# Products of two tiles in one VectorE instruction, and node comparisons moved to GpSimd, in the edge loop of a four-layer graph network

## The chip, the cores and the metric

The kernel runs on one core of one Trainium2 chip. The metric is the device time of one execution in microseconds, as the median of several runs.

## The reference, cut to what matters

Four graph layers follow each other on 1250 nodes with 512 features and 21250 edges (sorted by receiver). Each is added to its input and normalised. The change lies in the second layer, an equivariant message-passing layer, whose edge part is this:

```python
s0 = x0[sender]; s1 = x1[sender]                  # gathered rows: 128 and 3 x 128 numbers an edge
p1 = w1 * s0 * y0                                 # w1..w4: 4 x 128 weights an edge, h @ W_mlp4
p2 = (w2 * s0)[:, :, None] * y1[:, None, :]       # y0, y1: 1 + 3 numbers an edge
p3 = w3[:, :, None] * s1 * y0[:, None, :]
p4 = w4 * jnp.einsum('eum,em->eu', s1, y1) / SQRT3
msg0 = jax.ops.segment_sum(m0, receiver, num_segments=num_nodes)   # m0 = [p1, p4], m1 = [p2, p3]
msg1 = jax.ops.segment_sum(m1, receiver, num_segments=num_nodes)
```

## The kernel before, in words

The edges were sorted by the kernel itself into 208 tiles of 128 edges (`NT = G * GT`, 52 x 4). All edges of a tile have their receivers within one block of 32 nodes (`DB`). The edge loop walks over the tiles in steps of eight (`TP`): the loop body holds two steps (`par` 0 and 1), and there are 26 steps. All engines run their own stream and meet in semaphores.

For one tile m:

- GpSimd gathers the 128 sender rows of `xup` (512 numbers each) by an indirect DMA into slot m of `ring` (line 721, semaphore `s_gath[m]`). Before each step it copies the step's edge records into `gidx` and `gslot` (lines 710 and 711). Every second gather waits for `s_prod_ok`, that is until the products of the step before have left the two slots.
- TensorE computes the weights of two tiles at once, a pair (`tpw`, line 1102), into two PSUM banks: 0 and 1, or 6 and 7. `tpw` of a pair waits until the products two pairs earlier have read those banks.
- VectorE multiplies (`products`): line 2071 makes 2 x 128 products a lane, line 2072 makes 2 x 384 products a lane, from PSUM and `ring` into slot m mod 4 of `prod`. For every fourth tile it first compares the receivers of four tiles with 0 to 31 (line 2063, `eq4`).
- ScalarE scales the comparison result by the four y of each edge (line 1578, four instructions a tile, `sel4`).
- TensorE sums the tile's products by receiver with `sel4` as weights (`scat`, line 1116) into bank 2 + m mod 4. It waits for the tile's products and its `sel4`.
- VectorE adds the sum to the accumulator of the tile's node block (`add_sums`, line 2080). The block's number comes from a packed word which VectorE's sequencer loads once in four tiles (line 2090).

`add_sums` waits for two things: for its tile's `scat`, and for the addition of the tile before, because both may hit the same block of the accumulator:

```python
dve.wait_ge(s_scat_done, n + 5)
dve.wait_ge(s_gsum_ok, n + 4)
```

The order on VectorE before is: products of tile m + 3, addition of tile m, products of tile m + 4, addition of tile m + 1, and so on (`AHEAD = 3`). On TensorE it is, for each pair k: `tpw` of pair k + 1, then the two `scat` of pair k. Nothing of the rest of the kernel lies beside this loop: before it the node rows `xup` are written, and behind it TensorE waits for `s_acc_done`.

## Time and profile before

| | |
|---|---|
| median of 3 runs | 1691.36 us (1691.3 to 1697.8) |
| span of the profiled execution | 1690.4 us |
| PE busy | 1478.5 us |
| DVE busy | 1306.6 us |
| ACT busy | 739.0 us |
| POOL busy | 498.2 us |

The profiled execution is known by its span, 1690.4 us; the fastest of the three timed runs is 0.9 us longer than that, and the median 1.0 us. Busy time counts an engine's own instructions; the registers, waits and branches of its sequencer are not in it. Start times in the trace are counted from the span's start.

### The profile page before, as it was taken

The page shows a single profiled execution, that of the slowest core. Times are in us where ns is not written, and L with a number is a line of the kernel's source. Part 1 is how long each engine was busy: PE and PEld are TensorE (multiplying, and loading weights), DVE is VectorE, ACT ScalarE, POOL GpSimd, SP SyncE. Part 2 cuts the span into 40 slices and gives each one's busy share as a digit, 9 for nine tenths or more (in the row PEclk, how much of TensorE's full clock was granted, in tenths as well). Part 3 has the DMA queues.
Part 4 walks back from the last instruction along what each step waited for, and adds up shares of the span by engine and source line. Part 5 has one row for each costly group of instructions (what it writes and reads, how often), then busy time and mean ns, then how long its engine had stood idle before and what let it go on. Part 6 is the DMA issues. An engine that isn't in the chain of part 4 may idle for free.

```text
span 1690.4 us, 24268 instructions
## 1 busy us (share of the span) xinstructions
PE 1478.5 (87%) x7869; PEld 805.5 (48%) x7869; DVE 1306.6 (77%) x2051; ACT 739.0 (44%) x1580; POOL 498.2 (29%) x496
## 2 busy tenths in 40 slices
PE   2888998367888787899999999979999999999997
PEld 1465445213333335566555565855544444444443
DVE  8786999997999997499898999697577656632232
ACT  1285666267555555355454555441244333402000
POOL 1788888710011012356555664000000000002000
PEclk9988999678999997799999999979999999999999
DMA  4101000143121102466565667000111201220000
GB/s 143 42 6 9 6 7 7 36 146 114 43 68 40 65 16 82 129 184 183 165 183 165 182 184 148 1 1 26 50 50 50 70 30 58 66 74 1 13 19 30
DMA packets 66890, 122.06 MB, mean 72 GB/s; under 512 B 12753, under 2 KB 31299, under 8 KB 66702
## 3 DMA queue, kind: packets, MB, share of 16 engines
q0 software_dynamic: 23408, 59.71, 14.1%
q1 hardware_dynamic: 41976, 57.57, 10.5%
q10 hardware_dynamic: 1446, 4.03, 0.7%
q8 instruction: 31, 0.51, 0.1%
q14 instruction: 29, 0.24, 0.1%
HBM read 105.85 MB, written 15.23 MB: 72 GB/s over the span
## 4 chain that ended last, share of the span: by engine, by line
PE 53%; DVE 16%; POOL 14%; issue 10%; ACT 4%; DMA 2%; DVEq 1%; ACTq 0%; POOLq 0%
PE PS L1240 18%; POOL recs L656 14%; PE PS L1116 8%; DVE arena L1923 6%; PE PS L1205 5%; PE PS L1306 5%; PE PS L1102 5%; DVE arena L1919 3%; ACT arena L1578 3%; PE PS L1291 2%; PE PS L1302 2%; PE PS L1167 1%; DVE cnt_d L1704 1%; DVE arena L2123 1%; PE PS L976 1%
## 5 line engine op out<-in xcount | busy, mean ns | idle before, releaser
L1240 PE MATMUL PS<-arena 128*125 128x512 f32 x640 | 275.0, 592 | 0.0
L656 POOL DMA_INDIRECT recs<-arena x170 | 244.3, 1437 | 89.9 <-issue 89.0
L1578 ACT ACTIVATE arena<-arena,gslot 128x32 f32<-128x32 f32 x832 | 185.1, 308 | 172.5 <-PE PS L1116 89.6
L1116 PE MATMUL PS<-arena 128*32 128x128 f32 (+1 forms) x3328 | 235.0, 311 | 16.2 <-issue 8.0
L721 POOL DMA_INDIRECT arena<-xup,gidx x208 | 197.5, 949 | 147.6 <-issue 69.9
L1116 PEld LDWEIGHTS PS<-arena 128*32 128x32 f32 x3328 | 176.9, 111 | 127.1 <-issue 68.6
L1028 PE MATMUL PS<-arena 125*128 125x512 f32 (+1 forms) x480 | 190.5, 534 | 44.1 <-DVE arena L1923 43.9
L2072 DVE TENSOR_TENSOR arena<-PS,arena 128x768 f32<-128x768 f32 x208 | 196.7, 946 | 0.0
L1240 PEld LDWEIGHTS PS<-arena 128*125 128x125 f32 x640 | 120.1, 188 | 154.6 <-issue 154.1
L1028 PEld LDWEIGHTS PS<-arena 125*128 125x128 f32 x480 | 86.0, 191 | 148.4 <-issue 78.0
L728 POOL CAST arena<-cnt_s 125x1250 f32<-125x1250 uint16 x10 | 12.5, 1302 | 473.1 <-PE PS L1240 473.1
L1523 ACT ACTIVATE arena<-arena,c 125x1250 f32<-125x1250 f32 x80 | 106.8, 1337 | 101.2 <-DVE arena L1919 101.1
L1919 DVE SCALAR_TENSOR_TENSOR arena<-arena,c 125x1250 f32<-125x1250 f32 (+1 forms) x100 | 137.9, 1381 | 1.4 <-DVE c L1928 0.7
L1102 PE MATMUL PS<-arena 64*128 64x512 f32 x416 | 122.4, 660 | 1.8 <-issue 1.8
L1923 DVE SCALAR_TENSOR_TENSOR arena<-arena,cnt_s 125x1250 f32<-125x1250 f32 x80 | 116.0, 1451 | 0.0
L2071 DVE TENSOR_TENSOR arena<-PS,arena 128x256 f32<-128x256 f32 x208 | 86.5, 416 | 25.8 <-remote 9.8
L1660 ACT ACTIVATE arena<-arena,cslot 128x2500 f32<-128x2500 f32 x16 | 38.1, 2383 | 131.0 <-DVE cslot L2178 131.0
L1407 ACT ACTIVATE arena<-PS 125x626 uint16<-125x626 f32 x104 | 70.1, 692 | 57.4 <-PE PS L882 40.2
L2232 DVE TENSOR_SCALAR arena<-PS,deg 125x512 f32<-125x512 f32 x10 | 7.5, 751 | 111.9 <-PE PS L1306 111.9
L2080 DVE TENSOR_TENSOR arena<-PS,arena 128x256 f32 x208 | 85.7, 412 | 8.7 <-remote 7.6
L1306 PE MATMUL PS<-arena 125*125 125x512 f32 x200 | 87.5, 592 | 0.0
L1205 PE MATMUL PS<-arena,x_sb 125*128 125x512 f32 (+2 forms) x280 | 86.7, 471 | 0.0
(341 smaller groups left out, 2149.9 us busy)
## 6 DMA issues: line engine op xcount, KB each, us to landing
arena<-in_spline_wT SPq DMA_DIRECT2D x16, 1024.0 KB, 5.4
arena<-uv_rows SPq DMA_DIRECT2D x14, 610.4 KB
arena<-h_rows SPq DMA_DIRECT2D x26, 256.0 KB
h_rows<-arena SPq DMA_DIRECT2D x24, 256.0 KB, 2.8
arena<-xup,gidx POOLq DMA_INDIRECT x208
recs<-arena POOLq DMA_INDIRECT x170
xup<-arena SPq DMA_DIRECT2D x10, 250.0 KB
out<-x_sb SPq DMA_DIRECT2D x10, 250.0 KB
```

Source lines behind the costliest of these rows:

```text
L656: pool.indirect_dma_start(out=recs, out_offset=bass.IndirectOffsetOnAxis(pos[:, c:c + 1], 0), in_=rec[:, c, :], in_offset=None).then_inc(s ...
L721: pool.indirect_dma_start(out=ring[:, m, :], out_offset=None, in_=xup, in_offset=bass.IndirectOffsetOnAxis(gidx[:, par, m:m + 1], 0))\
L1028: ins = t.matmul(PS[:, 3 * par + q, 0:n1 - n0], hs[:, sblk, par * C:par * C + 2 * C], wt[:, sblk % WR, n0:n1], start=(sblk == 0), stop=(sb ...
L1102: t.matmul(PS[:, tpw_bank[(2 * k + q) % 4], :], h3[r, buf, k * 128:(k + 1) * 128], w_m4[r, :], start=True, stop=True, tile_position=(q * H ...
L1116: ins = t.matmul(PS[quad * DB:(quad + 1) * DB, bank, o0 * MUL:o0 * MUL + w], sel4[:, s, v * DB:(v + 1) * DB], prod[:, s, c0 * MUL:c1 * MUL ...
L1205: ins = t.matmul(PS[:, b0 + q, 0:n1 - n0], w, P50[:, k, n0:n1], start=(k == 0), stop=(k == NB - 1))
L1240: return t.matmul(PS[:NP, y2_bank(half, b), :], lhs[:, (k * HB + b) * NP:(k * HB + b + 1) * NP], w[:, k * D:(k + 1) * D], start=(first and ...
L1306: ins = t.matmul(PS[:NP, b % 2, :], cnt50[:, k, b * NP:(b + 1) * NP], z_sb[:, k, :], start=(k == 0), stop=(k == NB - 1))
L1578: ins = A(sel4[:, s, y * DB:(y + 1) * DB], eq4[:, m // 4, s * DB:(s + 1) * DB], ACT.Copy, scale=gslot[:, par, c + R_Y + y:c + R_Y + y + 1])
L1919: v.scalar_tensor_tensor(dst, U, cc, V, ALU.add, ALU.max).then_inc(ok, 1)
L1923: v.scalar_tensor_tensor(dst, e, 1.0, cm, ALU.min, ALU.mult).then_inc(ok, 1)
L2072: v.tensor_tensor(pr[:, :, 1:4, :], w[:, 1:4:2, :].unsqueeze(2).to_broadcast([128, 2, 3, MUL]), xg[:, 1:4, :].unsqueeze(1).to_broadcast([1 ...
```

## The change

Three things change in the edge loop:

- `products` becomes `pair_products`: lines 2071 and 2072 now cover both tiles of a pair, 4 x 128 and 4 x 384 products a lane, with one pair of instructions for two tiles. VectorE's order becomes: products of pair k + 1, addition of tile 2k, addition of tile 2k + 1.
- The comparison leaves VectorE. GpSimd makes it, tile by tile, for all eight tiles of a step, behind the step's second gather, into `eq8`.
- The other edits use one counting semaphore where several stood (`s_xt_cp`, `s_xt_ps`, `s_cols_cp`, `s_cols_ps`) and delete helper functions that nothing calls.

```diff
-        eq4 = at(22700, [128, 2, 4 * DB])
+        eq8 = at(22700, [128, 2, TP * DB])
@@ GpSimd, in the loop over the eight gathers of a step
+                        if m == 1:
+                            for q in range(TP):
+                                ins = pool.tensor_scalar(eq8[:, par, q * DB:(q + 1) * DB], iota_dst[:, 0:DB],
+                                                         gslot[:, par, q * RW + R_DL:q * RW + R_DL + 1], None, ALU.is_equal)
+                            ins.then_inc(s_eq_ok, 1)
@@ ScalarE
-                if m % 4 == 0:
-                    act.wait_ge(s_eq_ok, n4)
+                if m == 0:
+                    act.wait_ge(s_eq_ok, group)
@@ VectorE
-            def products(m, par, n, n_pair, n_gath):
...
-                v.tensor_tensor(pr[:, :, 0, :], w[:, 0:3:2, :], xg[:, 0:1, :].to_broadcast([128, 2, MUL]), ALU.mult)
-                v.tensor_tensor(pr[:, :, 1:4, :], w[:, 1:4:2, :].unsqueeze(2).to_broadcast([128, 2, 3, MUL]),
-                                xg[:, 1:4, :].unsqueeze(1).to_broadcast([128, 2, 3, MUL]), ALU.mult).then_inc(s_prod_ok, 1)
+            def pair_products(k, par, n, n_gath):
+
+                m, s = 2 * k, 2 * k % 4
+                xg = ring[:, m:m + 2, :].rearrange("p t (q n) -> p t q n", q=4)
+                b0 = (0, 6)[k % 2]
+                w = PS[:, b0:b0 + 2, :].rearrange("p t (h g n) -> p t h g n", h=2, g=2)
+                pr = prod[:, s:s + 2, :].rearrange("p t (h q n) -> p t h q n", h=2, q=4)
                 dve.wait_ge(s_gath[m], n_gath)
-                dve.wait_ge(s_tpw_ps, n + (2 - m % 2))
+                dve.wait_ge(s_gath[m + 1], n_gath)
+                dve.wait_ge(s_tpw_ps, n + 2)
+                v.tensor_tensor(pr[:, :, :, 0, :], w[:, :, :, 0, :], xg[:, :, 0:1, :].to_broadcast([128, 2, 2, MUL]), ALU.mult)
+                v.tensor_tensor(pr[:, :, :, 1:4, :], w[:, :, :, 1, :].unsqueeze(3).to_broadcast([128, 2, 2, 3, MUL]),
+                                xg[:, :, 1:4, :].unsqueeze(2).to_broadcast([128, 2, 2, 3, MUL]), ALU.mult).then_inc(s_prod_ok, 2)
@@ two_groups, VectorE
-                for m in range(TP):
-                    if m + AHEAD < TP:
-                        products(m + AHEAD, par, i * (2 * TP) + (TP * par + m + AHEAD), None, i * 32 + 16 * (par + 1))
+                for k in range(GT):
+                    if k + 1 < GT:
+                        pair_products(k + 1, par, i * (2 * TP) + (TP * par + 2 * k + 2), i * 32 + 16 * (par + 1))
...
-                    add_sums(m, i * (2 * TP) + (TP * par + m), word)
+                    for m in (2 * k, 2 * k + 1):
+                        add_sums(m, i * (2 * TP) + (TP * par + m), word)
```

On VectorE, inside the loop body, these rows stood one after another before: the products of a tile (lines 2071 and 2072), the registers and the addition of another tile (line 2080), and the same again. PS is PSUM; `arena` holds `prod`, `ring` and the accumulator.

```order
L2071 TENSOR_TENSOR arena<-PS,arena 128x2x128 [waits s_tpw_ps]
L2072 TENSOR_TENSOR arena<-PS,arena 128x2x384
L2080 REGISTER_ALU [waits s_gsum_ok,s_scat_done]
L2080 REGISTER_ALU
L2080 ISA
L2080 TENSOR_TENSOR arena<-PS,arena 128x256
L2071 TENSOR_TENSOR arena<-PS,arena 128x2x128 [waits s_tpw_ps,s_gath5]
L2072 TENSOR_TENSOR arena<-PS,arena 128x2x384
L2077 REGISTER_ALU
L2080 REGISTER_ALU [waits s_gsum_ok,s_scat_done]
```

At the same place of the changed kernel the products are lines 2040 and 2041 and the addition is line 2049.

```order
L2041 TENSOR_TENSOR arena<-PS,arena 128x4x384
L2058 ISA
L2058 TENSOR_LOAD gpk
L2058 ISA x2
L2046 REGISTER_ALU
L2049 REGISTER_ALU [waits s_gsum_ok,s_scat_done]
L2049 ISA
L2049 TENSOR_TENSOR arena<-PS,arena 128x256
L2046 REGISTER_ALU
L2049 REGISTER_ALU [waits s_gsum_ok,s_scat_done]
L2049 REGISTER_ALU
L2049 ISA
```

Two additions now stand behind each other with only register rows between them, and the second one waits for `s_gsum_ok`, which the first one raises; before, two product instructions stood between two additions.

On GpSimd, in the first step of the loop body of the changed kernel, the gathers are line 713:

```order
L703 COPY gslot<-gld 128x128
L704 ISA
L711 REGISTER_ALU [waits s_xup_out1,s_gidx_ok,s_xup_out0]
L713 DMA arena<-xup,gidx 128x512 [waits s_prod_ok]
L713 DMA arena<-xup,gidx 128x512
L718 TENSOR_SCALAR arena<-iota_dst,gslot 128x32 x8
L711 REGISTER_ALU
L713 DMA arena<-xup,gidx 128x512 [waits s_prod_ok]
```

The eight comparisons (line 718) stand between the second and the third gather; the row of eight was not there before, and the rest of GpSimd's order is as it was.

## Rows read from the trace of the kernel before

**Rows 1.** The page, part 1: busy time, share of the span, instructions of each engine.

```profile
PE 1478.5 (87%) x7869; PEld 805.5 (48%) x7869; DVE 1306.6 (77%) x2051; ACT 739.0 (44%) x1580; POOL 498.2 (29%) x496
```

**Rows 2.** Windows: length, busy time of PE, PEld, DVE, ACT, POOL, PEclk, DMA.

```profile
886.00:912.00 26.00, 22.83 (x220) 13.62 (x217) 20.18 (x43) 10.73 (x48) 12.84 (x16) 0.87 0.48 139
...
938.00:964.00 26.00, 25.48 (x290) 15.75 (x288) 25.34 (x53) 14.22 (x64) 15.72 (x21) 1.00 0.64 185
```

**Rows 3.** Groups by line and shape, 690 to 1060: busy, mean ns, idle before.

```profile
L2072 DVE TENSOR_TENSOR arena<-PS,arena 128x768 f32<-128x768 f32 x208 | 196.7, 946 | 0.0
L1578 ACT ACTIVATE arena<-arena,gslot 128x32 f32<-128x32 f32 x832 | 185.1, 308 | 172.5 <-PE PS L1116 89.6 <-DVE arena L2063 67.0 <-remote 15.8
...
L2071 DVE TENSOR_TENSOR arena<-PS,arena 128x256 f32<-128x256 f32 x208 | 86.5, 416 | 25.8 <-remote 9.8 <-DMA arena<-xup,gidx 7.8 <-PE PS L1102 5.1
L2080 DVE TENSOR_TENSOR arena<-PS,arena 128x256 f32 x208 | 85.7, 412 | 8.7 <-remote 7.6 <-DVE arena L2080 0.7 <-PE PS L1116 0.4
...
L2063 DVE TENSOR_TENSOR arena<-iota_dst,gslot 128x128 f32<-128x128 f32 x52 | 14.5, 280 | 4.7 <-POOL gslot L711 4.7
```

**Rows 4.** Timeline of DVE, four tiles of the steady loop: start, duration, instruction.

```profile
732.96 0.28 DVE L2063 TENSOR_TENSOR arena<-iota_dst,gslot 128x128 f32<-128x128 f32 x1
733.16 0.42 DVE L2071 TENSOR_TENSOR arena<-PS,arena 128x256 f32<-128x256 f32 x1
733.49 0.94 DVE L2072 TENSOR_TENSOR arena<-PS,arena 128x768 f32<-128x768 f32 x1
734.36 0.41 DVE L2080 TENSOR_TENSOR arena<-PS,arena 128x256 f32 x1
734.69 0.41 DVE L2071 TENSOR_TENSOR arena<-PS,arena 128x256 f32<-128x256 f32 x1
...
735.89 0.41 DVE L2080 TENSOR_TENSOR arena<-PS,arena 128x256 f32 x1
736.41 0.42 DVE L2071 TENSOR_TENSOR arena<-PS,arena 128x256 f32<-128x256 f32 x1
...
739.47 0.28 DVE L2063 TENSOR_TENSOR arena<-iota_dst,gslot 128x128 f32<-128x128 f32 x1
```

**Rows 5.** Timeline of DVE, the last additions of the loop.

```profile
1056.30 0.41 DVE L2080 TENSOR_TENSOR arena<-PS,arena 128x256 f32 x1
1057.07 0.42 DVE L2080 TENSOR_TENSOR arena<-PS,arena 128x256 f32 x1 [0.36 <-DVE arena L2080]
1057.86 0.42 DVE L2080 TENSOR_TENSOR arena<-PS,arena 128x256 f32 x1 [0.36 <-PE PS L1116]
1058.65 0.42 DVE L2080 TENSOR_TENSOR arena<-PS,arena 128x256 f32 x1 [0.36 <-DVE arena L2080]
```

**Rows 6.** Timeline of PE, 904 to 912, behind a stall of its own.

```profile
905.11 1.13 PE L1102 MATMUL PS<-arena 64*128 64x512 f32 x4
906.17 1.96 PE L1116 MATMUL PS<-arena 128*32 128x256 f32 x32
908.06 1.13 PE L1102 MATMUL PS<-arena 64*128 64x512 f32 x4
```

**Rows 7.** Timeline of POOL, one step of eight tiles.

```profile
735.80 0.28 POOL L711 COPY gslot<-gld 128x128 f32<-128x128 f32 x1
736.96 0.97 POOL L721 DMA_INDIRECT arena<-xup,gidx  x1 [0.87 <-issue]
738.23 0.95 POOL L721 DMA_INDIRECT arena<-xup,gidx  x1 [0.30 <-issue]
739.97 0.94 POOL L721 DMA_INDIRECT arena<-xup,gidx  x1 [0.79 <-DVE arena L2072]
...
743.23 0.94 POOL L721 DMA_INDIRECT arena<-xup,gidx  x1 [1.06 <-DVE arena L2072]
...
746.50 0.95 POOL L721 DMA_INDIRECT arena<-xup,gidx  x1 [1.08 <-issue]
...
748.85 0.28 POOL L711 COPY gslot<-gld 128x128 f32<-128x128 f32 x1
```

**Rows 8.** Groups of POOL by shape, whole span.

```profile
L710 POOL COPY gidx<-gld 128x8 uint32<-128x8 uint32 x26 | 5.2, 199 | 39.6 <-DVEq L2052 39.5
...
L643 POOL TENSOR_SCALAR_AFFINE_SELECT upper<-upper 128x128 f32<-128x128 f32 x1 | 0.3, 282 | 0.0
```

**Rows 9.** VectorE's sequencer, loop branch: duration ns min/median/max, first and last start.

```profile
L2095 DVEq FUSED_REGOPS  x12: 62/63/70, 701.6 to 1009.0; - x12
...
L2095 DVEq COMPARE_BRANCH  x12: 50/56/74, 736.9 to 1034.8; - x12
```

More of the change, by code:

```diff
@@ L733, in _ @@
             t = nc.tensor
-            def transposes(src, ready, done, copied, banks, copied0=0):
-                for b in range(NB):
-                    if ready is not None:
-                        pe.wait_ge(*ready(b))
-                    if b >= 2:
-                        pe.wait_ge(copied, copied0 + b - 1)
-                    for k in range(KT):
-                        ins = t.transpose(PS[:, banks[b % 2], k * 128:k * 128 + NP], src(b, k), ident[:NP, :NP])
-                    ins.then_inc(done, 1)
-            def node_product(lhs, rhs, nk, done, copied, banks, cols=D):
-                for b in range(NB):
-                    if b >= 2:
-                        pe.wait_ge(copied, b - 1)
-                    for k in range(nk):
-                        ins = t.matmul(PS[:NP, banks[b % 2], 0:cols], lhs(b, k), rhs(k), start=(k == 0), stop=(k == nk - 1))
-                    ins.then_inc(done, 1)
-            def blk_of(v):
-                return lambda b, k: v[:, k, b * NP:(b + 1) * NP]
             def uv_transposes(src, nr, done, b0):
@@ L1053, in x1_transposes @@
                     ins = t.transpose(PS[:, 4 + b % 2, k * 128:k * 128 + NP], src, ident[:NP, :NP])
-                ins.then_inc(s_xt1_ps, 1)
+                ins.then_inc(s_xt_ps, 1)
             def linear_up(b):
-                pe.wait_ge(s_xt1_cp, b + 1)
+                pe.wait_ge(s_xt_cp, NB + b + 1)
                 if b == 0:
@@ L1174, in _ @@
                 x2_transposes(b)
-            pe.wait_ge(s_xt2_cp, NB - 1)
+            pe.wait_ge(s_xt_cp, 3 * NB - 1)
             quad_rows(wa2, xT2, 0, 0, s_r4_ps)
             quad_rows(wa2, xT2, 1, 1, s_r4_ps)
-            pe.wait_ge(s_xt2_cp, NB)
+            pe.wait_ge(s_xt_cp, 3 * NB)
             quad_rows(wa2, xT2, 2, 2, s_r4_ps)
@@ L1282, in _ @@
             for c in range(NB):
-                pe.wait_ge(s_xt3_cp, c + 1)
+                pe.wait_ge(s_xt_cp, 3 * NB + c + 1)
                 if c == 0:
@@ L1320, in ln_sqrt, with evac_T @@
                 A(rstd[:, b:b + 1], mv[:, b, 1:2], ACT.Sqrt, bias=epsc[:NP, :]).then_inc(s_ln_sd, 1)
-            def evac_T(dst, done, copied, banks, layer=0, then=None):
+            def evac_T(dst, done, copied, banks, n0, layer, then):
                 if layer:
@@ L1329, in evac_T @@
                         ln_sqrt(layer, b + 1)
-                    act.wait_ge(done, b + 1)
+                    act.wait_ge(done, n0 + b + 1)
                     A(dst[:, :, b * NP:(b + 1) * NP],
@@ L1569, in _, with scaled_onehots @@
             A(w_o0[:, 1, :], w_o0[:, 1, :], ACT.Copy, scale=3.0 ** -0.5).then_inc(s_wo_ok, 1)
-            def scaled_onehots(m, par, n, n4):
+            def scaled_onehots(m, par, n, group):
                 s, c = m % 4, m * RW
-                if m % 4 == 0:
-                    act.wait_ge(s_eq_ok, n4)
+                if m == 0:
+                    act.wait_ge(s_eq_ok, group)
                 act.wait_ge(s_scat_done, n + 1)
                 for y in range(4):
-                    ins = A(sel4[:, s, y * DB:(y + 1) * DB], eq4[:, m // 4, s * DB:(s + 1) * DB], ACT.Copy,
+                    ins = A(sel4[:, s, y * DB:(y + 1) * DB], eq8[:, par, m * DB:(m + 1) * DB], ACT.Copy,
                             scale=gslot[:, par, c + R_Y + y:c + R_Y + y + 1])
```

61 lines of the change are left out of this document (19 added, 42 removed).

## The prediction

> **What bounds the kernel now.** The page's busy shares come first [rows 1]: TensorE 87%, VectorE 77%. They are means over stages, so they don't say who sets the pace of the edge loop; the views of the stretch from 690 to 1060 us do. In a steady window of 26 us VectorE is busy 25.34 us, at TensorE's full clock (1.00) [rows 2]. That window holds sixteen tiles. TensorE's busy time is as high, 25.48 us, but overlapping matmuls fill it, so I read its pace elsewhere. In the timeline of VectorE [rows 4] one instruction starts as the one before ends: from one comparison to the next, four tiles later, 739.47 - 732.96 = 6.51 us pass, of which about 0.2 us is idle. Behind a stall of its own, when it has work waiting, TensorE takes 908.06 - 905.11 = 2.95 us for a pair [rows 6], that is 5.90 us for four tiles. ScalarE is busy for 185.1 us of some 360 [rows 3]. So VectorE sets the pace with 6.51 us, TensorE is only 0.6 us behind it, and a gain on VectorE can be worth 0.6 us in four tiles at most, 52 x 0.6 = 31 us in all. In a few stretches TensorE stalls on itself and VectorE runs at 20.18 of 26 us [rows 2]; there the change is worth nothing. I count 5 of the 52 fours as lost to those and 47 as set by VectorE.
>
> **The pieces of VectorE's 6.51 us.** Starts matter here, not durations, since an instruction starts some 0.08 us before the one in front is over. From [rows 4]: 2071 to 2072 takes 733.49 - 733.16 = 0.33 us, 2072 to 2080 0.87, 2080 to 2071 734.69 - 734.36 = 0.33, comparison to 2071 0.20. Four tiles are 4 x 1.53 = 6.12, plus the comparison 0.20, plus one gap: between 735.89 and 736.41 there are 0.52 instead of 0.33, 0.19 more. Sum 6.51. I don't know the gap's cause for certain; the group view puts 5.1 us before 2071 down to `tpw` [rows 3].
>
> **The change, part by part.**
>
> *Longer products.* 256 elements take 0.33 us and 768 take 0.87: 0.54 us for 512 more, 1.05 ns an element, and so about 0.06 us fixed an instruction. A pair's first instruction has 512 elements, 0.33 + 0.27 = 0.60 us; the second 1536, 0.87 + 0.81 = 1.68. Together 2.28 against 2 x 1.20 = 2.40 before. The saving is 0.12 a pair, 0.24 in four tiles. The Trainium skill ("VectorE: DVE Perf Modes", on the errata mechanism) also says that many small tiles each pay a bubble which one large tile pays once.
>
> *Comparison gone from VectorE.* 0.20 us less in four tiles.
>
> *Two additions side by side.* Here the order shown above matters more than the instruction count. The second addition of a pair waits for the first one to be finished. Before, the products of another tile lay between, 1.20 us, and hid that wait: 2080 shows 0.7 us of waits for 2080 in the whole loop [rows 3]. The last additions of the loop, where no products are left, show the wait bare [rows 5]: starts at 1056.30, 1057.07, 1057.86, 1058.65, that is 0.77 to 0.79 us apart with 0.36 us idle, instead of 0.33. (The view names TensorE for one of the three; the distance is the same, so I read all three as the addition's own chain through the sequencer.) I take 0.78, so 0.45 more a pair, 0.90 in four tiles. Behind it on VectorE's queue stand the next pair's products, for which the gathers and TensorE's `scat` wait.
>
> A page speaks against this step. The Trainium skill ("VectorE: DVE Perf Modes", The DRAIN you can't avoid) measured a chain of copies as no slower with a semaphore behind each than with one at the end. By that rule the wait would be free, and the time would be that of the first rival below, 1666 us; these rows, in which the next instruction waits for that semaphore, show 0.36 us of idle time.
>
> *Sum for four tiles:* 6.51 - 0.24 - 0.20 + 0.90 = 6.97, with the gap of 0.19 kept. If the gap goes, 6.78. The gap is a wait for TensorE, which gets more room now, but I can't show that it goes: bounds 6.78 and 6.97, and I take 6.87. Against 6.51 that is +0.36 (+0.27 to +0.46), times 47: +17 us (+13 to +22).
>
> *The loop's branch.* Before, its sequencer work ran while products were under way. Now the loop body ends on an addition that was issued only just in time, so the branch and the registers behind it come ahead of the next products. Branch and register row take 0.056 + 0.063 = 0.12 us [rows 9], twelve times: +1.4 us. The lower bound is 0; for the upper I take the idle time that a late-issued addition shows, 0.36 us [rows 5], twelve times, 4.3 us. I take 2.
>
> *Entry and end.* The first products now wait for two gathers, which start 1.27 us apart when they don't wait (736.96 and 738.23, [rows 7]). So 0 to 1.3 us; VectorE waits later for TensorE at the entry anyhow, so I take 0. The last four additions were a chain before and still are: 0.
>
> *GpSimd's eight comparisons.* No row shows this operation. The nearest are a copy of 8 columns, 0.20 us, and a select of 128 columns, 0.28 us [rows 8]; 32 columns lie between, 1.6 to 2.3 us for eight. Is there room? A step takes 748.85 - 735.80 = 13.05 us, and the three waits in it are 0.79, 1.06 and 1.08 where a gather that doesn't wait shows 0.30 [rows 7]. Room is 0.49 + 0.76 + 0.78 = 2.0 us, and the work 11.0. At the new pace of 2 x 6.87 = 13.7 us there is 2.7, so up to 0.34 us each is hidden. The third and fourth gather of a step leave about 1 us later, but they are needed six tiles after their slot is freed, over 9 us. ScalarE needs the comparisons only once the step before has come to its fifth `scat`, some 6.9 us after the release of the first gather; two gathers (2.5) and 2.3 of comparisons are done by then. Cost 0. Without this cover it is the second rival.
>
> *TensorE.* `scat` of both tiles of a pair now starts at the end of the pair's products, then comes the next `tpw`: 2.95 us of work within a pair's 3.4. That hides with 0.4 us to spare. The merged semaphores and deleted helpers issue nothing in other places: 0.
>
> **Sum:** 17 + 2 = +19 us on the profiled execution, 1690.4 + 19 = 1709. The median of the runs lies 1.0 us above that span. I rounded the terms no finer than that, and predict 1710 us.
>
> **The rivals.**
>
> *The additions do not cost more* (the wait is overlapped, as the page's rule has it). Then four tiles need 6.87 - 0.90 = 5.97 on VectorE and 5.90 on TensorE: 0.54 less than 6.51, times 47 = -25 us, 1666 us. For it: the group view shows hardly any such wait. Against it: that view's additions stood apart, and three of three that stand together show it. It decides below a distance of 0.60 us between two additions: 0.33 + (6.51 - 5.97) / 2; above that the old 6.51 isn't undercut. Chance 0.12. Between the two, an extra of 0.1 to 0.3 us in place of 0.45, or a gap that vanishes along with less waiting than I think, gives 1683 to 1699: 0.20.
>
> *GpSimd becomes the bound.* If a comparison costs 0.5 us, a step is 11.0 + 4.0 = 15.0 us against 13.0: 26 x 2.0 = +52, 1743 us. For it: its instruction with a per-edge operand is shown nowhere. Against it: every small operation in its rows is under 0.3. It decides above 0.34 us. Chance 0.06.
>
> *More waits for TensorE.* The pair has one product instruction instead of two to be released, and the next pair's `tpw` lies behind both `scat`. If the gap came at each pair instead of each second one: another 0.19 x 47 = +9, and with the branch at its upper bound 1722 us. Chance 0.08.
>
> My own forecast, 1700 to 1717: 0.54.
>
> **How the numbers follow.** About 0.5%, 8.5 us, is what a measurement of this kernel tells from no change. Faster by more than that: the first rival and a small part of the cases between, 0.15. Within 0.5%, 1683 to 1700: most of the between cases and the lower edge of mine, 0.20. Slower: 0.65. The range leaves out the first rival and GpSimd's case (0.12 and 0.06): 1682 to 1726 us. The likeliest case alone is 1700 to 1717.
>
> **What the profile after would show.** VectorE: additions in twos, 0.78 us apart with some 0.36 us idle in the second, about 104 times, so close to 37 us of idle time before the addition, put down to the addition itself. Product instructions of about 0.68 and 1.75 us (start distances plus 0.08). Four tiles in 6.8 to 7.0 us. VectorE's busy time falls by 0.44 x 52 = 23 us although the span grows. GpSimd: comparisons of 0.2 to 0.28 us and gathers that still wait for the products. ScalarE: no waits for `s_eq_ok` in the steady loop. Wrong would be: additions 0.33 us apart, comparisons above 0.34 us, or a granted clock of TensorE that falls in the steady windows, for which nothing here gives a reason.

## The result, and the profile after

The changed kernel takes 1780.2 us (median of 4 runs, 1776.7 to 1785.1) beside 1692.6 us for the kernel before: ratio 1.052, interval 1.049 to 1.056, 88 us slower. Forecast were 1710 us, in a range of 1682 to 1726.

The page of the kernel after, part 1, on its profiled execution (span 1783.6 us), as in [rows 1]:

```profile
PE 1488.8 (83%) x7869; PEld 808.6 (45%) x7869; DVE 1288.7 (72%) x1791; ACT 746.8 (42%) x1580; POOL 575.6 (32%) x704
```

VectorE is busy 17.9 us less than before and the span is 93 us longer, so it waits more. For what, the groups of the loop say (690 to 1150 us, by shape, as in [rows 3]):

```profile
L713 POOL DMA_INDIRECT arena<-xup,gidx x208 | 200.4, 963 | 161.2 <-DVE arena L2041 96.4 <-issue 62.1 <-POOL gslot L703 2.7
...
L2041 DVE TENSOR_TENSOR arena<-PS,arena 128x1536 f32<-128x1536 f32 x103 | 180.1, 1749 | 0.0
...
L2049 DVE TENSOR_TENSOR arena<-PS,arena 128x256 f32 x204 | 85.8, 421 | 125.4 <-remote 93.5 <-DVE arena L2049 27.5 <-PE PS L1091 4.3
L2040 DVE TENSOR_TENSOR arena<-PS,arena 128x512 f32<-128x512 f32 x104 | 71.0, 683 | 23.0 <-DMA arena<-xup,gidx 16.9 <-remote 3.3 <-issue 2.5
```

The 27.5 us in which the addition (L2049) waits for itself were forecast. The 93.5 us were not; the view of the waits counts them as 26, which is about one for each of the 26 steps of eight tiles. "Remote" names no engine: the view found no instruction that had ended shortly before the wait did. The timelines of one stretch show what happened. First VectorE:

```profile
1010.64 0.42 DVE L2049 TENSOR_TENSOR arena<-PS,arena 128x256 f32 x1 [0.36 <-DVE arena L2049]
1010.99 0.68 DVE L2040 TENSOR_TENSOR arena<-PS,arena 128x512 f32<-128x512 f32 x1
1011.58 1.75 DVE L2041 TENSOR_TENSOR arena<-PS,arena 128x1536 f32<-128x1536 f32 x1
1013.25 0.42 DVE L2049 TENSOR_TENSOR arena<-PS,arena 128x256 f32 x1
1017.91 0.42 DVE L2049 TENSOR_TENSOR arena<-PS,arena 128x256 f32 x1 [4.24 <-remote]
```

A pair without a disturbance takes 3.38 us (from 1007.26, not shown, to 1010.64); this one takes 7.27. TensorE, whose `scat` (L1091) an addition waits for, in the same time (x is the number of instructions in a row):

```profile
1011.97 1.13 PE L1077 MATMUL PS<-arena 64*128 64x512 f32 x4
1013.46 0.97 PE L1091 MATMUL PS<-arena 128*32 128x256 f32 x15 [0.37 <-DVE arena L2041]
1014.72 0.27 PE L1091 MATMUL PS<-arena 128*32 128x128 f32 x1 [0.29 <-issue]
1015.43 0.38 PE L1091 MATMUL PS<-arena 128*32 128x256 f32 x1 [0.44 <-issue]
1016.14 0.62 PE L1091 MATMUL PS<-arena 128*32 128x256 f32 x4 [0.34 <-issue]
1017.56 1.60 PE L1091 MATMUL PS<-arena 128*32 128x128 f32 x11 [0.79 <-issue]
1019.09 2.08 PE L1077 MATMUL PS<-arena 64*128 64x512 f32 x4
```

The 16 `scat` matmuls of the second tile need 4.4 us instead of 1.0. Between them TensorE waits for nothing that the profile knows ("issue"): it starts one every 0.7 us. The `tpw` behind them takes 2.08 us instead of 1.13. In the window from 1018 to 1020 us the granted clock is 0.50, that is 1.2 GHz instead of 2.4; in the two windows of 2 us before, TensorE was busy for 1.08 and 1.06 us.

These starts are not yet what VectorE waits for. The addition that starts at 1017.91 needs the sums of a pair whose `scat` TensorE began at 1010.08 and, by the record, ended at 1012.03. But the ends of matmuls in the profile are modelled; the trace also holds the time of each semaphore signal, and there the signal of that `scat` stands at 1017.62, which is 5.6 us later. The `scat` of the tile before it was signalled at 1012.53, 1.4 us late, and none between the two. ScalarE, which waits for the same signals, starts at the same two moments:

```profile
1012.55 0.96 ACT L1553 ACTIVATE arena<-arena,gslot 128x32 f32<-128x32 f32 x4 [2.84 <-PE PS L1091]
1017.65 2.67 ACT L1553 ACTIVATE arena<-arena,gslot 128x32 f32<-128x32 f32 x12 [4.13 <-remote]
```

VectorE's own signals are on time in this stretch (product ends 1013.33, signal 1013.34). So it is TensorE that falls behind, and it does so before its starts show it. Of its 208 `scat` signals 26 come more than 4 us behind the recorded end. And GpSimd:

```profile
1003.94 0.97 POOL L713 DMA_INDIRECT arena<-xup,gidx  x1 [4.31 <-DVE arena L2041]
1005.22 0.95 POOL L713 DMA_INDIRECT arena<-xup,gidx  x1 [0.30 <-issue]
1006.20 2.72 POOL L718 TENSOR_SCALAR arena<-iota_dst,gslot 128x32 f32<-128x32 f32 x8
1009.08 1.04 POOL L713 DMA_INDIRECT arena<-xup,gidx  x1 [0.16 <-issue]
1010.42 0.94 POOL L713 DMA_INDIRECT arena<-xup,gidx  x1 [0.30 <-issue]
...
1014.18 0.94 POOL L713 DMA_INDIRECT arena<-xup,gidx  x1 [0.30 <-issue]
1015.43 0.95 POOL L713 DMA_INDIRECT arena<-xup,gidx  x1 [0.30 <-issue]
```

Eight comparisons in 2.72 us make it late. What its gathers wait for has then long happened, so six follow each other 1.25 to 1.34 us apart. Before, they mostly came in twos with a pause [rows 7]. TensorE's signals are late from the second of the six on (start 1010.42; the signal due at 1011.16 comes at 1012.53), its starts falter from the fifth on, and it recovers 1.2 us after the sixth has been issued. After a stall GpSimd waits for the slots to come free (4.31 us ahead of this step, 96.4 us in the loop), and the next step begins in the same way.

The kernel before has this too, where I had counted 5 of the 52 fours as lost without asking why. GpSimd and TensorE there (timelines; they lie in the first window of [rows 2], whose mean clock is 0.87):

```profile
888.62 0.94 POOL L721 DMA_INDIRECT arena<-xup,gidx  x1 [2.07 <-DVE arena L2072]
889.87 0.95 POOL L721 DMA_INDIRECT arena<-xup,gidx  x1 [0.30 <-issue]
...
896.13 0.95 POOL L721 DMA_INDIRECT arena<-xup,gidx  x1 [0.31 <-issue]
```

```profile
894.32 0.66 PE L1102 MATMUL PS<-arena 64*128 64x512 f32 x1 [0.47 <-issue]
895.73 1.01 PE L1102 MATMUL PS<-arena 64*128 64x512 f32 x1 [0.75 <-issue]
897.12 0.58 PE L1116 MATMUL PS<-arena 128*32 128x256 f32 x1 [0.39 <-issue]
```

Seven gathers 1.25 us apart, and TensorE starts one matmul every 1.4 us. Theory A was therefore: GpSimd's lateness makes a run of five or more gathers without a pause, and such a run slows TensorE. Rivals: B, the pair products; C, the comparisons as work of GpSimd's, wherever they stand; D, ScalarE waiting for their result. (The theories go by TensorE's starts, not by its signals.)

### The profile page after: what moved, and what is told of

It reads as the page before. It is cut to its first block, busy times and chain, and to the rows that moved or that the text cites. A ratio compares the mean times of both kernels' runs of the same rounds, so it can differ in the third digit from the quotient of the medians.

```text
span 1783.6 us, 24120 instructions
## 1 busy us (share of the span) xinstructions
PE 1488.8 (83%) x7869; PEld 808.6 (45%) x7869; DVE 1288.7 (72%) x1791; ACT 746.8 (42%) x1580; POOL 575.6 (32%) x704
## 4 chain that ended last, share of the span: by engine, by line
PE 43%; DVE 22%; POOL 13%; issue 12%; another core or an unknown queue 4%; DVEq 2%; DMA 2%; ACT 2%; POOLq 0%; ACTq 0%
PE PS L1215 17%; POOL recs L648 13%; DVE arena L2041 7%; DVE arena L1898 6%; PE PS L1091 6%; PE PS L1281 5%; PE PS L1180 5%; DVE arena L1894 3%; PE PS L1266 2%; PE PS L1277 2%; DVE arena L2049 1%; DVEq L2049 1%; PE PS L1142 1%; DVE cnt_d L1679 1%
## 5 line engine op out<-in xcount | busy, mean ns | idle before, releaser
L1091 PE MATMUL PS<-arena 128*32 128x128 f32 (+1 forms) x3328 | 241.3, 309 | 95.3 <-issue 48.8
L1553 ACT ACTIVATE arena<-arena,gslot 128x32 f32<-128x32 f32 x832 | 192.2, 311 | 255.8 <-PE PS L1091 129.1
L1091 PEld LDWEIGHTS PS<-arena 128*32 128x32 f32 x3328 | 184.1, 110 | 213.5 <-issue 122.2
L648 POOL DMA_INDIRECT recs<-arena x170 | 247.9, 1458 | 89.9 <-issue 89.3
L713 POOL DMA_INDIRECT arena<-xup,gidx x208 | 200.4, 963 | 161.2 <-DVE arena L2041 96.4
L2041 DVE TENSOR_TENSOR arena<-PS,arena 128x1536 f32<-128x1536 f32 x104 | 181.8, 1749 | 0.0
L2049 DVE TENSOR_TENSOR arena<-PS,arena 128x256 f32 x208 | 87.5, 421 | 126.5 <-remote 93.5
L2040 DVE TENSOR_TENSOR arena<-PS,arena 128x512 f32<-128x512 f32 x104 | 71.0, 683 | 23.0 <-DMA arena<-xup,gidx 16.9
```

The costliest lines, as they stand in the source:

```text
L648: pool.indirect_dma_start(out=recs, out_offset=bass.IndirectOffsetOnAxis(pos[:, c:c + 1], 0), in_=rec[:, c, :], in_offset=None).then_inc(s ...
L713: pool.indirect_dma_start(out=ring[:, m, :], out_offset=None, in_=xup, in_offset=bass.IndirectOffsetOnAxis(gidx[:, par, m:m + 1], 0))\
L1091: ins = t.matmul(PS[quad * DB:(quad + 1) * DB, bank, o0 * MUL:o0 * MUL + w], sel4[:, s, v * DB:(v + 1) * DB], prod[:, s, c0 * MUL:c1 * MUL ...
L1553: ins = A(sel4[:, s, y * DB:(y + 1) * DB], eq8[:, par, m * DB:(m + 1) * DB], ACT.Copy, scale=gslot[:, par, c + R_Y + y:c + R_Y + y + 1])
L2041: v.tensor_tensor(pr[:, :, :, 1:4, :], w[:, :, :, 1, :].unsqueeze(3).to_broadcast([128, 2, 2, 3, MUL]), xg[:, :, 1:4, :].unsqueeze(2).to_b ...
```

## Experiments

In the edits, "new" is the changed kernel and "old" the one before. Kernels of one group ran on one chip; ratios are against the kernel before on that chip.

**The two halves apart, and idle work** (kernel before: 1691.5 us).

`e1_pairs_only` is new with the comparisons on VectorE, one instruction for four tiles:

```diff
-  if m == 1:   # GpSimd, behind the second gather
-      for q in range(TP): ins = pool.tensor_scalar(eq8[...q...], iota_dst, gslot[...q...], None, ALU.is_equal)
+  if k % 2 == 0:   # VectorE, pair_products
+      v.tensor_tensor(eq8[... 4 tiles], iota_dst..., dl..., ALU.is_equal).then_inc(s_eq_ok, 1)
```

> The change's products of two tiles, but the comparisons back on VectorE, four tiles an instruction as before. Theory A (TensorE's slow stretches come from runs of back-to-back gathers, which GpSimd's 2.7 us of comparisons cause): no such runs, so few slow stretches, and only the forecast cost of the two additions side by side is left: 6.78 us for four tiles plus the comparison's 0.20, 1705 to 1718 us. Rival B (the stretches come from the pair products, since TensorE now waits for one long release instead of two): about 1780 us.

Measured: 1710.9 us, ratio 1.014 (1.008 to 1.020). No stall in every step. Its additions as forecast (timeline of VectorE):

```profile
946.51 0.41 DVE L2052 TENSOR_TENSOR arena<-PS,arena 128x256 f32 x1
947.28 0.42 DVE L2052 TENSOR_TENSOR arena<-PS,arena 128x256 f32 x1 [0.36 <-DVE arena L2052]
```

`e2_compare_only` is old with the eight comparisons on GpSimd, the products tile by tile as before:

```diff
-  VectorE: v.tensor_tensor(eq4..., ALU.is_equal)   # four tiles
+  GpSimd:  if m == 1: for q in range(TP): pool.tensor_scalar(eq8[...q...], ..., ALU.is_equal)
```

> The kernel before with only the comparisons moved to GpSimd, eight behind the second gather. Theory A: VectorE saves 0.2 us in four tiles, but the slow stretches of TensorE come, 50 to 90 us more than before: 1735 to 1775 us. Rival B: about 10 us faster than before, 1682 us.

Measured: 1768.9 us, ratio 1.047 (1.042 to 1.052). The large loss comes with the comparisons and not with the pairs: B falls.

`e4_idle_work` is old with its comparisons left on VectorE, and eight more on GpSimd that nobody reads:

```diff
+  if m == 1:
+      for q in range(TP): pool.tensor_scalar(eqd[...q...], iota_dst, gslot[...q...], None, ALU.is_equal)
```

> The kernel before, with eight comparisons more on GpSimd behind the second gather of each step, written to a tile that nobody reads; VectorE and ScalarE are as before. Theory A: the delay alone makes the runs of gathers and with them the slow stretches: 1740 to 1790 us. Rival D (it is ScalarE's or TensorE's dependence on GpSimd's comparison result that stalls): 1691 us, no change.

Measured: 1777.5 us, ratio 1.053 (1.048 to 1.059). D falls: nobody waits for these results.

`e3_spread` is new with two comparisons behind every second gather:

```diff
-  if m == 1: for q in range(TP): ...
+  if m % 2 == 1: for q in (m - 1, m): ...
```

> The changed kernel with the same 208 comparisons on GpSimd, but two behind every second gather instead of eight behind the second gather of a step. Theory A: 0.7 us fits in GpSimd's wait for products, gathers stay in twos, few slow stretches, 1700 to 1712 us. Rival C (it is the work of the comparisons on GpSimd as such, its total or its traffic, that slows the loop): about 1780 us, as the total is unchanged.

Measured: 1697.4 us, ratio 1.004 (1.002 to 1.007), a little below the forecast. As many comparisons, and 83 us less than new took in its own group. GpSimd's timeline shows why: no gather but the second of a pair follows without other work.

```profile
950.54 0.74 POOL L718 TENSOR_SCALAR arena<-iota_dst,gslot 128x32 f32<-128x32 f32 x2
951.44 1.04 POOL L713 DMA_INDIRECT arena<-xup,gidx  x1 [0.16 <-issue]
952.78 0.95 POOL L713 DMA_INDIRECT arena<-xup,gidx  x1 [0.30 <-issue]
953.75 0.73 POOL L718 TENSOR_SCALAR arena<-iota_dst,gslot 128x32 f32<-128x32 f32 x2
```

**The dose, and how much the gathers carry** (another chip; kernel before: 1689.8 us).

`e9_four_and_four` is new with four comparisons behind the second gather and four behind the sixth; `e10_idle_work_spread` is `e4_idle_work` with two idle comparisons behind every second gather:

```diff
e9:  -  if m == 1: for q in range(TP): ...
     +  if m % 4 == 1: for q in range(m - 1, m + 3): ...
e10: -  if m == 1: for q in range(TP): ...
     +  if m % 2 == 1: for q in (m - 1, m): ...
```

> The changed kernel, with four comparisons behind the second and four behind the sixth gather of a step. GpSimd is late by 4 x 0.36 = 1.4 us twice a step instead of by 2.9 once. Theory A: fewer gathers follow each other without a wait (three or so instead of six), so the stretches are rare: between the 1697 us of two by two and the 1780 of eight together, and nearer to the first, 1695 to 1720. Rival (each comparison costs TensorE something by itself, wherever it stands): 1765 to 1785.

Measured: 1705.7 us, ratio 1.008 (1.005 to 1.011). Up to four gathers stand in a row in it. Behind one such row of four (starts 743.43 to 747.27) TensorE's starts falter from 747.70 on and an addition waits 2.9 us; the additions' other waits are 2.35 us (at 907 us, behind another row of four) and under 1 us. So four in a row are not always harmless.

> The kernel before, in which GpSimd also does eight comparisons a step that nobody reads, two behind every second gather. The same work eight together behind the second gather took 1777.5 us. Theory A: the gathers keep their distance, the stretches are those of the kernel before, and GpSimd has no room left: 1688 to 1700 us. Rival (the work itself disturbs, by a port or by the instruction's kind): 1765 to 1785 us.

Measured: 1698.2 us, ratio 1.007 (1.004 to 1.010). The same work eight together cost 86 us, two by two 8 us. C falls.

`e5_narrow_gathers` is new, each gather fetching 64 of the 512 numbers of a row.

```diff
+  pool.memset(ring[:], 0.0)
-  pool.indirect_dma_start(out=ring[:, m, :], in_=xup, ...)
+  pool.indirect_dma_start(out=ring[:, m, 0:64], in_=xup.rearrange("n (a b) -> (n a) b", b=64), ...)
```

> The changed kernel, with the eight comparisons behind the second gather as it has them, but each gather fetches 64 of the 512 numbers of a row into the first eighth of its slot; the other numbers of the ring are zero from one memset before the loop (an estimate of 3.5 us). Left out: seven eighths of each gathered row, so the messages are not the reference's. GpSimd's instructions are as many and in the same order, so the gathers still follow each other six in a row behind the comparisons. Theory A (TensorE slows down because a run of gathers moves over 200 GB/s): the stretches with one TensorE instruction every 0.7 us are gone, and the time is that of the pair products alone or a little above, 1700 to 1715 us. Rival (it is the issuing of gathers back to back by GpSimd, or their descriptors, whatever they move): the stretches stay, 11 or so of them, 1770 to 1785 us.

Measured: 1786.3 us, ratio 1.055 (1.052 to 1.059). The theory as the expectation states it, that the moved bytes do it, falls. From the windows of this kernel (length, busy time of PE, PEld, DVE, ACT, POOL, PEclk, DMA share, GB/s), during one of its stalls:

```profile
967.00:969.00 2.00, 1.63 (x10) 0.47 (x8) 0.86 (x1) 0.00 (x0) 1.33 (x2) 1.00 0.47 137
969.00:971.00 2.00, 1.30 (x12) 0.48 (x8) 0.42 (x1) 0.75 (x4) 1.69 (x4) 1.00 0.09 16
```

TensorE starts 10 and 12 instructions in 2 us, where new starts 34 from 1010 to 1012 us, ahead of its stall, while the DMA engines move 137 and 16 GB/s; in the stall of new shown above, 1014 to 1016 us, they move 238 GB/s. It isn't the bytes.

**Which part of the run does it.** Three variants: `e12_run_broken` is new with two more idle comparisons behind the sixth gather; `e13_run_without_gathers` is new in which an addition of 128x512 numbers on GpSimd takes the place of gathers 3 to 8 of a step; in `e14_quarter_rows` each gather fetches 32 rows instead of 128, into a ring that was zeroed.

```diff
e12: +  if m == 5:
     +      for q in range(2): pool.tensor_scalar(eqd[...], iota_dst, gslot[...], None, ALU.is_equal)
e13: +  if m >= 2: pool.tensor_tensor(ring[:, m, :], gslot..., gslot..., ALU.add).then_inc(s_gath[m], 16)
e14: -  pool.indirect_dma_start(out=ring[:, m, :], ... gidx[:, par, m:m + 1] ...)
     +  pool.indirect_dma_start(out=ring[0:32, m, :], ... gidx[0:32, par, m:m + 1] ...)
```

> The changed kernel, all eight comparisons behind the second gather as it has them, and two more comparisons that nobody reads behind the sixth gather: GpSimd does more work than in the changed kernel (0.7 us a step), but its run of six gathers is now one of four and one of two. Theory A2 (TensorE slows down from the fifth gather of a run without a wait on, whatever the gathers carry): the stall of 3.6 us in every step goes, and GpSimd's own work, 8 x 1.27 + 10 x 0.36 + 0.5 = 14.3 us a step against some 14, becomes the limit: 1700 to 1725 us, faster than the 1780 of the changed kernel although it does more. Rival (the stall comes from GpSimd being 2.9 us late once a step, by itself): no better than 1780, rather 1785 to 1800.

> The changed kernel, in which GpSimd adds two vectors of 128x512 numbers of its own into the slots of tiles 3 to 8 of a step instead of gathering them (left out: three quarters of the gathers; those tiles' messages are not the reference's). GpSimd is as late and has a run of six instructions without a wait, but of arithmetic; an estimate of 0.6 to 1.2 us each. Theory A2 (the run of gather issues slows TensorE): no slow stretch in the loop, 1690 to 1712 us. Rival (GpSimd busy without a pause, whatever it does): a stall in every step, 1760 to 1785 us.

> The changed kernel, but each gather fetches the rows of the first 32 edges of its tile instead of all 128; the rest of the ring is zero from one memset before the loop (left out: the messages of three quarters of the edges). As many gathers in the same order, with a quarter of the descriptors each. If it is the descriptors that GpSimd writes (128 a gather, run of six) that slow TensorE, the stalls shrink or go: 1700 to 1730 us. If it is the number of gather instructions in a row, 1770 to 1785 us. An issue that is much shorter than 0.95 us would end the run of six as well, and is then the reason.

Measured: 1712.7, 1686.8 and 1693.5 us, ratios 1.030 (1.025 to 1.036), 1.014 (1.009 to 1.019), 1.019 (1.014 to 1.024), and no stalls in any of them. But the kernel before took 1661.7 us beside them instead of 1690. So new was run again beside them, on yet another chip (kernel before: 1663.0 us); c2, c3 and c4 are e12, e13 and e14 unchanged.

> The changed kernel once more, as the measure for the three that run beside it. In the last batch the kernel before took 1661.7 us instead of 1690, which is 28 us less; so it is open whether the stalls arise on every chip. Theory A2 (stall behind a run of six gathers, everywhere): ratio 1.05 and a stall of 3.6 us in every step. Rival (the stalls belong to some chips only): beside a kernel before of 1662 us it shows none, ratio 1.01 to 1.02; beside one of 1690 us it shows them, ratio 1.05.

> The run of six gathers broken by two idle comparisons, again, beside the changed kernel. If the changed kernel shows stalls here and this one none, and the time is lower although GpSimd does more (1710 to 1730 us beside 1780), the run of gathers is the cause. If both show stalls, or neither, this kernel doesn't tell it.

> Arithmetic in the place of six of eight gathers, again, beside the changed kernel (left out: those gathers; their tiles' messages are not the reference's). If the changed kernel shows stalls here and this one none (1685 to 1715 us beside 1780), it is the gathers and not GpSimd being busy without a pause. If it shows them too, it is GpSimd's business or its lateness.

> Gathers of 32 rows instead of 128, again, beside the changed kernel (left out: the messages of three quarters of the edges). The issue stays 0.88 us, and the run of six gathers stays. Stalls gone beside a changed kernel that shows them (1690 to 1715 us beside 1780): it is what the gathers' rows make, their descriptors or packets. Stalls there too: it is the instructions.

Measured: the changed kernel itself 1697.6 us, ratio **1.020** (1.016 to 1.025); the others 1711.1, 1684.9 and 1699.6 us (1.027, 1.011, 1.021). GpSimd and TensorE of the changed kernel on this chip:

```profile
946.47 1.04 POOL L713 DMA_INDIRECT arena<-xup,gidx  x1 [0.16 <-issue]
947.81 0.95 POOL L713 DMA_INDIRECT arena<-xup,gidx  x1 [0.30 <-issue]
...
951.57 0.95 POOL L713 DMA_INDIRECT arena<-xup,gidx  x1 [0.30 <-issue]
952.82 0.95 POOL L713 DMA_INDIRECT arena<-xup,gidx  x1 [0.30 <-issue]
```

```profile
950.37 1.95 PE L1091 MATMUL PS<-arena 128*32 128x256 f32 x32 [0.36 <-DVE arena L2041]
952.25 1.13 PE L1077 MATMUL PS<-arena 64*128 64x512 f32 x4
```

The same six gathers in the same rhythm, and TensorE does its 32 `scat` matmuls in 1.95 us; all 208 of its `scat` signals come 0.01 us behind the recorded end. So there are two kinds of chip here: on one (the result and the first two groups of experiments, kernel before 1690 to 1693 us) such a run stalls TensorE, on the other (1662 to 1663 us) it doesn't. Each chip was met in one group only, so "kind" may as well be a condition that a chip was in at that time; no run separates the two. These two groups say nothing on which part of the run stalls TensorE, and e12, the broken run, was never tried on the first kind. e13 and e14, as d1 and d2, then met a chip of the first kind (kernel before: 1690.1 us):

> Arithmetic of GpSimd in the place of six of eight gathers (left out: those gathers; their tiles' messages are not the reference's), once more, in the hope of a chip that shows the stalls: one on which the kernel before takes about 1690 us, not 1662. On two chips of the fast kind it and the changed kernel alike showed none. On a chip with stalls: if the gathers of the run make them, none here, 1690 to 1712 us, ratio 1.00 to 1.013. If GpSimd being late and busy without a pause makes them, one in every step, ratio 1.04 to 1.055. On a chip of the fast kind it tells nothing new (ratio 1.01).

> Gathers of 32 rows instead of 128 in an unchanged order (left out: the messages of three quarters of the edges), once more, in the hope of a chip that shows the stalls. There: if it is what the rows make (their descriptors, their packets, in all a quarter as many), no stall or a small one, 1690 to 1720 us, ratio 1.00 to 1.018. If it is the gather instructions in a row, which stay 1.17 us apart, a stall in every step, ratio 1.04 to 1.055. On a chip of the fast kind it tells nothing new (ratio 1.02).

Measured: without gathers in the run 1686.8 us, ratio 0.998 (0.997 to 1.000), no stall. With a quarter of the rows 1785.4 us, ratio 1.058 (1.056 to 1.060). TensorE's timeline in this second one, gathers 1.17 to 1.23 us apart from 940.0 to 943.6 and again from 945.2:

```profile
944.55 0.64 PE L1094 MATMUL PS<-arena 128*32 128x256 f32 x10 [0.37 <-issue]
945.62 0.60 PE L1094 MATMUL PS<-arena 128*32 128x128 f32 x4 [0.44 <-issue]
947.09 0.27 PE L1094 MATMUL PS<-arena 128*32 128x128 f32 x1 [0.86 <-issue]
947.83 0.27 PE L1094 MATMUL PS<-arena 128*32 128x128 f32 x1 [0.47 <-issue]
```

So neither bytes nor rows: what matters is that gather instructions follow each other. Two gathers alone already do a small part of it. d1 has only two in a step, at 945.70 and 947.05 here; the `scat` signal due at 947.02 comes at 948.61, 1.6 us late, the next ones are on time again, and 21 of its 208 signals are over 1 us late, none over 1.65. ScalarE shows it: in d1 it has to stop for that signal between the scalings of two tiles, while in c3, the same kernel on a chip of the second kind, all eight instructions behind the first gather (948.46) run in a row. ScalarE in d1:

```profile
946.31 0.96 ACT L1558 ACTIVATE arena<-arena,gslot 128x32 f32<-128x32 f32 x4 [1.67 <-PE PS L1096]
948.63 0.96 ACT L1558 ACTIVATE arena<-arena,gslot 128x32 f32<-128x32 f32 x4 [1.37 <-remote]
```

And in c3:

```profile
948.95 1.83 ACT L1558 ACTIVATE arena<-arena,gslot 128x32 f32<-128x32 f32 x8 [1.55 <-PE PS L1096]
```

On the first kind of chip, then, a pair of gathers puts TensorE 1 to 1.6 us behind, and in the pause behind the pair it catches up; six in a row leave it no time for that.

That GpSimd is late and busy isn't enough, with one reserve: its additions take 1.01 us each and not 1.25, so after four of them it had caught up and waited 0.5 to 0.8 us. It was busy for 6.8 us without a pause behind its second gather, against 10 in new.

**A better order of the pair.** `e8_additions_between` has the comparisons on VectorE as `e1_pairs_only`, and the order: long product, addition 2k, short product, addition 2k+1.

```diff
-  product 512; product 1536 (raises s_prod_ok); addition 2k; addition 2k+1
+  product 1536; addition 2k; product 512 (raises s_prod_ok); addition 2k+1
```

> Pair products, but the two additions of the pair before stand between and behind the two product instructions (long product, addition, short product, addition), and the comparisons are back on VectorE, four tiles in one instruction; GpSimd has gathers alone. If an addition waits 0.45 us only because it stands right behind the other one, that goes: VectorE needs 0.60 + 1.68 + 2 x 0.33 = 2.94 us a pair, 0.1 more for the comparisons, about 3.0, and TensorE's 2.95 is the next limit. Against the 3.26 of before: 0.25 less times some 94 pairs, 1666 to 1675 us. Rival 1 (the short product waits for the addition or the addition for the product on the way, 0.36 us as between two additions): no better than 3.3 a pair, 1690 to 1700 us. Rival 2 (a faster VectorE frees slots sooner, GpSimd's gathers bunch up and TensorE's slow stretches return): 1700 us or more, and the stretches would be seen behind runs of gathers without a wait.

Measured (first kind of chip, kernel before 1689.8 us): 1726.6 us, ratio 1.021 (1.018 to 1.024). This forecast missed by over 50 us. The additions waited for TensorE, 30.7 us by "remote" and 25.5 by name in the loop: an addition asks for sums whose `scat` has only just been released, and part of these signals are late as above (recorded end 945.94, signal 947.51, addition 947.80). `e11_additions_later` puts each odd addition one place later, behind the next pair's long product; it also waits for `s_scat_done` ahead of the long product, and its first step stands outside the loop:

```diff
-  product 1536 (k+1); addition 2k;   product 512 (k+1); addition 2k+1
+  product 1536 (k+1); addition 2k-1; product 512 (k+1); addition 2k
```

> As the kernel with the additions between the products, but each odd addition stands one place later, behind the next pair's long product (long product, odd addition of the pair before last, short product, even addition). There an addition did wait for TensorE, for 30.7 + 25.5 us in the loop, since its tile's sums had only just been asked for. If that was what cost, VectorE waits only for the slots of the products before the long one: 3.1 to 3.2 us a pair, 1675 to 1690 us. Rival (TensorE itself needs over 3.3 us a pair once it is asked this early, or ScalarE's copies behind the later comparison do): 1700 to 1730 us, no better than 1726.

Measured, on a chip of the second kind only: 1653.4 us beside 1661.7, ratio 0.996 (0.993 to 0.998). Its timeline of VectorE shows the pair in 2.93 to 3.2 us, without a wait between additions:

```profile
950.91 1.75 DVE L2044 TENSOR_TENSOR arena<-PS,arena 128x1536 f32<-128x1536 f32 x1
952.58 0.41 DVE L2056 TENSOR_TENSOR arena<-PS,arena 128x256 f32 x1
952.91 0.68 DVE L2048 TENSOR_TENSOR arena<-PS,arena 128x512 f32<-128x512 f32 x1
953.51 0.41 DVE L2056 TENSOR_TENSOR arena<-PS,arena 128x256 f32 x1
953.84 1.75 DVE L2044 TENSOR_TENSOR arena<-PS,arena 128x1536 f32<-128x1536 f32 x1
```

It is the only version here that does the reference's whole work and is faster than the kernel before on its own chip, by 8 us. `e8_additions_between` and this one never ran on the same kind of chip, so how much of their difference comes from the order, and how much from signals that are on time here, is not shown; nor was it tried where gathers stall TensorE.

## Why the prediction was wrong

**Longer products, additions side by side, the gap:** right. The products take 0.68 and 1.75 us, the additions stand 0.78 us apart with 0.36 idle, the gap of 0.19 has gone, a pair takes 3.38, so four tiles 6.76. The branch costs 0.34 us, not 0.12: once in sixteen tiles a pair takes 3.72 us. That is 4 us in the loop, near my upper bound, and 0.085 in four tiles, which gives 6.85; I had taken 6.87 without the branch. VectorE's busy time fell by 17.9 us, not 23.

The idle 0.36 us is not the semaphore's price. In all 105 such gaps of the loop of `c1_after_again` (37.3 us in the 103 that the view puts down to the addition) 0.04 us pass from the end of the first addition to the wait instruction of VectorE's sequencer, and 0.32 us from there to the start of the second addition, with three register instructions in between, which work out the block's address. They stand behind the wait. The view of the addition's line in the changed kernel lists them (DVEq is VectorE's sequencer; durations in ns):

```profile
L2049 DVEq ALU_OP  x364: 40/45/57, 709.7 to 1154.0; - x182
L2049 DVEq FUSED_REGOPS  x208: 57/57/57, 709.8 to 1154.1; - x104
```

So the case doesn't contradict what the Trainium skill measured ("VectorE: DVE Perf Modes", The DRAIN you can't avoid): a semaphore behind each copy costs nothing extra there, and here 0.04 of the 0.36 us. What didn't hold was my step from there to the first rival. Working the address out ahead of the wait might save most of the 0.32 us; no run here tries it.

**"GpSimd's eight comparisons ... Cost 0":** this step failed, in three places. First the price: 0.36 us each (359 ns over 208), not 0.20 to 0.28, and above my own limit of 0.34, one of the listed signs of being wrong. Second the timing: "the third and fourth gather of a step leave about 1 us later" looked at two gathers. The third starts 3.86 us behind the second instead of 1.74 [rows 7], and since GpSimd doesn't catch up before the step ends, all six go out without a pause. Third, and this is the cost: I asked only when the gathers are needed. On this kind of chip the gathers themselves slow TensorE, and a run of six without a pause puts it 5 us behind; the prediction had no term for that, neither here nor under TensorE, whose work it let hide "with 0.4 us to spare". None of its rivals named it, and the one on GpSimd priced lateness by its busy time, 1743 us at 0.5 us each. Two more of its signs failed. ScalarE does wait for the comparisons in the loop (73.6 us in 25 waits in `c1_after_again`), though the additions wait for TensorE for only 0.8 us there, so it cost VectorE next to nothing. And the granted clock does fall, to 0.50 behind some of the stalls.

**What the terms measured.** On chips without stalls the change costs 34.6 us (1697.6 - 1663.0; by the interval of the ratio 26 to 41) where 19 were forecast. Chips of the two kinds differ by 82.6 us for the changed kernel (1780.2 - 1697.6) and by 29.6 for the one before (1692.6 - 1663.0), so stalls cost it 53.0 us more, and 34.6 + 53.0 = 87.6, the whole difference; this splits it and proves nothing. The traces agree in size with the 82.6: from 690 to 1150 us VectorE's additions and first products are preceded by 148.4 us of idle time in the changed kernel (125.4 + 23.0) and by 62.0 in `c1_after_again` (38.1 + 23.9), 86.4 less. That the forecast had the sign right says nothing for this part of it: on a chip with stalls most of the loss comes from what it had put at 0.

**Open.** Of the 34.6 us, 52 times 0.34 us (6.85 - 6.51) are 18. For the rest there are two candidates that no run separates. The first is gathers that come late. VectorE's first product of a pair waits 22.3 us for them in `c1_after_again`. Of these 13.9 are the one wait at the loop's start, which was there before as well (4.7 ahead of the comparison and 7.4 ahead of the product, 12.1 together). The next, 3.1 us, is for the third and fourth gathers, which now stand behind the eight comparisons; the entry had been put at 0 to 1.3 us. The remaining 5.3 us lie in the loop. The second is that the kernel before was profiled on a chip with stalls alone. Its gap of 0.19 us may come from TensorE's late signals; without it four tiles would take 6.32 us, an estimate from [rows 4], and the change would cost 52 x 0.19 = 10 us more on the other kind of chip. With the 18 and some 5 to 10 us for the gathers that gives 33 to 38 us by estimate, but no profile of the kernel before on such a chip exists. That `e1_pairs_only` came out at the predicted 1710 us is partly chance: it has one stall in the steady loop (at 904 us), where the kernel before has two of about 4 us (at 825 and 899 us) and the forecast had taken them to stay. Why a gather slows TensorE, and why on some chips only, no run here shows.

## What to carry to other kernels

Work that is put on an engine which issues transfers delays them, and a delayed engine then issues them in one go, without the pauses in which others catch up: ask for the rhythm of its queue, not only for its free time and for when the data is needed. Idle comparisons two by two behind every second gather cost 8 us, the same eight together 86. A stretch that is lost in the kernel before has a cause, which the change can make frequent; look at what every other engine did just ahead of it. Where a wait is put down to "remote", compare the time of the signal with the recorded end of the instruction that raises it: TensorE's recorded ends can be microseconds early. Count the register instructions that stand behind a wait as part of its price. And run the changed kernel again beside its variants when the kernel before comes out at another time.

## What was unexpected of the hardware

- On some chips GpSimd's gathers slow TensorE. Two put its `scat` signals 1.0 to 1.6 us behind the recorded ends (the changed kernel, `d1_run_without_gathers`), six in a row, 1.17 to 1.34 us apart, 5.6 us. From the fourth or fifth gather of a run on (747.70 in `e9_four_and_four`, 944.55 in `d2_quarter_rows`, 1014.72 in new) it also starts only one instruction every 0.7 us or so, or every 1.4 us in the kernel before, without any wait that the profile knows. GpSimd's own fifth gather can be late too: it starts 1.59 us behind the fourth in `d2_quarter_rows`, with no wait named. 128 rows of 2 KB, 128 of 256 bytes, or 32 of 2 KB make little difference (ratios 1.052, 1.055, 1.058). Behind some stalls the granted clock falls to 0.50 (1018 to 1020 us in new), behind others it stays at 1.00 (the one that ends at 1035 us).
- It depends on the chip, or on a condition that a chip is in. The variants ran on three chips with stalls; on a fourth the changed kernel has the same instructions at the same distances and none, and on a fifth the kernel before was as fast as there.
- The issue of a gather takes 0.95 us for 128 rows and 0.87 for 32. The Trainium skill ("Perfetto Trace Analysis", DMA Instruction — SWDGE (GPSIMD)) says that the profile's end of such an instruction is the end of making descriptors and not of moving data. If so, 96 rows more cost 0.08 us and nearly all of the time is fixed.
- A comparison of 128x32 numbers with one number per partition takes GpSimd 0.36 us, more than the 0.28 us of a select of four times as many columns [rows 8].
